# A decoder layer's self attention on one Trainium2 core: projection weights held while two batches' tokens stream

## The chip, the core and the metric

The kernel runs on one core of one Trainium2 chip. The metric is the device time of one execution in microseconds. Times named here are of one profiled execution unless the text says that they are the median of several runs.

## What is computed

One decoder layer in fp32 for 8 batches of 112 tokens of width 512: self attention, then cross attention over 375 context rows of width 128, then a mixture of experts, each behind a layer norm and each added to its input. Cut to what the change touches:

```python
def self_attention(x, Wq, Wk, Wv, Wp):          # x: [8, 112, 512], normed
    Q = (x @ Wq.T).reshape(B, T, 16, 32).transpose(0, 2, 1, 3)
    K = (x @ Wk.T).reshape(B, T, 4, 32).transpose(0, 2, 1, 3)
    V = (x @ Wv.T).reshape(B, T, 4, 32).transpose(0, 2, 1, 3)
    Q, K = apply_rope(Q), apply_rope(K)          # halves of 16: x1 cos - x2 sin, x2 cos + x1 sin
    scores = einsum('bkgtd,bksd->bkgts', Q.reshape(B, 4, 4, T, 32), K) / sqrt(32)
    attn = softmax(where(causal, scores, lowest))
    return einsum('bkgts,bksd->bkgtd', attn, V) -> [B, T, 512] @ Wp.T

def cross_attention(hidden, kv_c, Wq, w_kc_q, w_kc_kv, W_qr, W_kr, Wo):   # 16 heads
    q_big = einsum('bshk,hkq->bshq', hidden @ Wq.T, w_kc_q)
    scores = einsum(q_big @ W_qr, kv_rope @ W_kr)  # per head, over 375 context rows
    ...
```

## The kernel before

The engines' programs are written out by hand, one function per engine, and each engine runs its instructions in exactly the order of that function. They meet by semaphores only. The part around the change is the block of self attention, from about 10 to 165 us of the span. It runs in `ROUNDS` = 4 rounds; round i treats two batches, q = 0 and 1. The loop `for i in range(ROUNDS)` in each engine's program sets the order of the work.

**Projection.** Token rows are layer-normed (`first_norm`, L1613 on DVE gives `xn`), turned by PE (`turn_x`) into `xt_hl`: ACT copies a high part, DVE subtracts to get a low part. The weights `wqkv_hl` are split in the same way, and a product is three matmuls, high by high, high by low, low by high (`mm3`, L62 to L64). These operands have the type fp32r, a rounded fp32; other matmuls here take plain fp32, and one such instruction shows as two records in the profile. `project_qkv(i, q)` holds one batch's 112 tokens in the array and streams weights past them: 12 matmuls of 512 columns for the queries, 12 of 256 for keys and values. The results lie with tokens on partitions.

**Rotary embedding.** `rope` on DVE (L1634 to L1637, six multiplications a batch), `rope_add` on POOL (L2116, L2119, two additions of 512 elements a batch), then `turn_qk` turns queries and keys on PE (8 transposes a batch, L741), and ACT copies them to SBUF (`copy_qk`, L1234). ACT copies the values (`copy_v`, L1227).

**Scores and softmax.** `scores` adds the mask by a bf16 matmul (L824) and 16 matmuls on tiles of 32 rows (L829). On DVE `shift` takes the largest value (L1646) and subtracts it (L1648), ACT takes the exponential (`exp`, L1238), DVE sums (L1653), POOL normalises (L2126). A round's probabilities are used in the next round: `turn_probs` (L848, four groups of four transposes, ACT copies each, L1245), `apply_probs` (L858), `heads_high` on ACT (L1250) and `heads_low` on DVE (L1658) split the result, `project_out` (24 matmuls of 512 columns for both batches), `turn_x2` turns the next norm's output.

**Weights of the cross attention,** made in the same loop: round i treats the pairs of heads p = 2i and 2i+1. `scores_weight` (L750) gives `m_sb`, `out_weight` (L757) gives `bw_sb`, `query_weight` (L764) multiplies `m_sb` by the query weight, ACT copies the result (`at_sb`), `turn_query_weight` (L771) turns it on PE, and DVE or ACT copies it into `aw_sb`. `turn_context` (L778) and `context_turned_low` (L1684) prepare the context rows of one batch (`kvt_hl`).

Four PSUM banks hold scores and, between two scores, the weights of the cross attention (`s_ps`); `f_ps` (two banks) holds projections and their turned forms; `k_ps` (two banks, also `b_ps`) holds turned probabilities, heads and the output projection.

Of the kernel before, what the change touches and what calls it, by code (L numbers as in the profile page):

```python
# [12 lines left out]
F32 = mybir.dt.float32  # L13
F32R = mybir.dt.float32r
# [270 lines left out]
def attention(nc, a, sem, sb, ctx, ident, x_all, x_sb, xn2_hl, w_raw, p_raw, mask, stats_all, ow_dram, kvn_dram, kvt_dram, aw_dram,  # L285
# [30 lines left out]
    with ExitStack() as room:  # L316
        wqkv_hl = sb("wqkv_hl", [128, 2, KC, QKV], F32R, room)
        xt_hl, xn = pairs("xt_hl", [128, 2, KC, T], F32R, room), pairs("xn", [T, C], F32, room)
# [8 lines left out]
    with ExitStack() as room:  # L327
# [4 lines left out]
        at_sb, aw_sb, bw_sb = sb("at_sb", [128, C], F32, room), sb("aw_sb", [128, C], F32, room), sb("bw_sb", [128, 2, C], F32, room)  # L332
# [20 lines left out]
    with ExitStack() as room:  # L353
        qcos, qsin = sb("qcos", [T, HD], F32, room), sb("qsin", [T, HD], F32, room)
        mask_bf, ident_bf = sb("mask_bf", [T, PER, T], BF16, room), sb("ident_bf", [T, T], BF16, room)
        rq, rt = pairs("rq", [T, C], F32, room), pairs("rt", [T, C], F32, room)
        rk, rkt = pairs("rk", [T, GROUPS, PER, HD], F32, room), pairs("rkt", [T, 2, GROUPS, HD], F32, room)
        qt, kt = sb("qt", [128, KC, T], F32, room), sb("kt", [128, KC, T], F32, room)
# [18 lines left out]
    with ExitStack() as room:  # L377
        wp_hl, x2n = sb("wp_hl", [128, 2, KC, C], F32R, room), pairs("x2n", [T, C], F32, room)
        v_sb = [sb(f"v_sb{z}", [T, GROUPS, HD], F32, room) for z in range(4)]
# [49 lines left out]
    tab_loaded, mask_loaded, setup = sem("tab_loaded"), sem("mask_loaded"), sem("setup")  # L429
# [5 lines left out]
    at_done, at_copied, ta_done, a_ready = sem("at_done"), sem("at_copied"), sem("ta_done"), sem("a_ready")  # L435
# [10 lines left out]
    qkv_done, v_copied = sem("qkv_done"), sem("v_copied")  # L446
    rope_read, roped = sem("rope_read"), sem("roped")
    qkt_done, qkt_copied = sem("qkt_done"), sem("qkt_copied")
# [12 lines left out]

    def is_last(i):
        return i == ROUNDS

# [112 lines left out]
    with nc.Block() as block:  # L577
        @block.sync
        def _(sp):
# [53 lines left out]
            sp.dma_start(qcos[:, :], a["qcos"]).then_inc(tab_loaded, 16)  # L633
            sp.dma_start(qsin[:, :], a["qsin"]).then_inc(tab_loaded, 16)
# [12 lines left out]
            for p in range(PAIRS):  # L647
# [7 lines left out]
                if p + 1 < PAIRS:  # L655
                    sp.wait_ge(at_done, p + 1)
                    load_q(p + 1)
# [15 lines left out]
                if p == 5:  # L673
                    sp.wait_ge(a_stored, 16 * 4)
                    sp.wait_ge(qkv_done, 2 * B)
# [62 lines left out]
        def _(pe):  # L738
# [4 lines left out]

            def scores_weight(p):
# [14 lines left out]
            def query_weight(p):  # L759
# [8 lines left out]
            def turn_query_weight(p):  # L768
# [2080 lines left out]
```

## Time and profile before

| quantity | value |
|---|---|
| time, median of 3 runs (lowest, highest) | 562.0 us (561.52, 563.93) |
| profiled execution | 559.57 us, span 557.7 us |
| busy PE | 528.3 us (95%) |
| busy PEld (weight load) | 375.9 us |
| busy DVE | 400.5 us |
| busy ACT | 302.9 us |
| busy POOL | 281.3 us |
| mean granted clock of TensorE | 0.998 |

The span is the first to the last instruction; the execution's own time has 1.87 us around it. PE is busy for nearly all of the span, and its overlapped weight loads (PEld) are counted apart. In the table of 40 slices PE stands at 9 tenths or more in nearly all slices behind the first three. The self-attention block is slices 1 to 12.

### The profile page before, as it was taken

How to read it: one execution, taken by the hardware profiler on the slowest of the kernel's cores; microseconds unless marked ns; L12 is line 12 of the kernel's file. 1: busy time of each engine (PE TensorE's matmuls, PEld its weight loads, DVE VectorE, ACT ScalarE, POOL GpSimd, SP SyncE). 2: the span in 40 equal slices, each digit the busy share in tenths (PEclk: the TensorE clock that was granted, in tenths of full speed). 3: DMA queues.
4: the chain of work that ended last, by engine and by line, in shares of the span. 5: the costliest groups of instructions: out<-in, count | busy, mean ns of one | idle time of the engine just before them, and what ended most of it. 6: DMA issues, size and time to landing. Idle time of an engine off the chain costs nothing. (4 is left out here: it accounts for less than half of the span.)

```text
span 557.7 us, 9735 instructions
## 1 busy us (share of the span) xinstructions
PE 528.3 (95%) x3451; PEld 375.9 (67%) x3451; DVE 400.5 (72%) x912; ACT 302.9 (54%) x693; POOL 281.3 (50%) x359
## 2 busy tenths in 40 slices
PE   5989999999989999999999999999999999998996
PEld 4657776767767676576666776677678766884443
DVE  5675798797586698866877468894576667786873
ACT  3164735735655677655776456775466653622430
POOL 0579643564715776812666215693154552572650
PEclk9999999999999999999999999999999999999999
DMA  8976645766451630233693333244030019125828
GB/s 242 273 259 229 225 137 162 270 182 205 178 168 56 167 135 2 38 88 121 173 278 92 79 95 84 42 77 76 0 115 9 0 35 419 35 82 108 214 87 263
DMA packets 46194, 76.64 MB, mean 137 GB/s; under 512 B 20066, under 2 KB 30084, under 8 KB 45252
## 3 DMA queue, kind: packets, MB, share of 16 engines
q1 hardware_dynamic: 42948, 63.60, 36.8%
q0 software_dynamic: 2176, 10.60, 8.6%
q10 hardware_dynamic: 1024, 1.84, 1.0%
q8 instruction: 28, 0.46, 0.3%
q14 instruction: 18, 0.15, 0.1%
HBM read 57.36 MB, written 28.10 MB: 153 GB/s over the span
## 5 line engine op out<-in xcount | busy, mean ns | idle before, releaser
L2133 POOL TENSOR_TENSOR xprob<-xprob,erec 128x375 f32<-128x375 f32 x112 | 93.8, 843 | 129.4 <-DVE erec L1751 129.1
L1340 ACT ACTIVATE xprob<-s_ps,nmax 128x375 f32<-128x375 f32 x112 | 64.2, 573 | 55.0 <-DVE nmax L1746 53.2
L1746 DVE TENSOR_REDUCE nmax<-s_ps 128x1 f32<-128x375 f32 x112 | 59.5, 538 | 0.0
L2126 POOL TENSOR_TENSOR prob<-prob,rec 112x1792 f32<-112x1792 f32 x8 | 25.5, 3183 | 51.4 <-DVE rec L1654 51.2
L62 PE MATMUL s_ps<-kvt,qt_hl 128*128 128x376 f32 x112 | 48.1, 429 | 2.0 <-ACT xprob L1340 1.3
L1729 DVE SCALAR_TENSOR_TENSOR pt_hl<-f_ps,pt_hl 125x384 f16<-125x384 f32 (+1 forms) x62 | 38.0, 614 | 13.9 <-ACT pt_hl L1318 12.6
L62 PE MATMUL k_ps<-ow,ctx_hl 128*128 128x512 f16 (+1 forms) x104 | 39.6, 381 | 0.0
L64 PE MATMUL k_ps<-ow,ctx_hl 128*128 128x512 f16 (+1 forms) x104 | 39.4, 379 | 0.0
L63 PE MATMUL k_ps<-ow,ctx_hl 128*128 128x512 f16 (+1 forms) x104 | 39.4, 379 | 0.0
L63 PE MATMUL s_ps<-kvt,qt_hl 128*128 128x376 f32 x112 | 37.4, 334 | 0.0
L64 PE MATMUL s_ps<-kvt,qt_hl 128*128 128x376 f32 x112 | 37.4, 334 | 0.0
L1737 DVE SCALAR_TENSOR_TENSOR ctx_hl<-k_ps,ctx_hl 128x448 f16<-128x448 f32 (+1 forms) x32 | 18.7, 584 | 25.8 <-ACT ctx_hl L1326 23.6
L1318 ACT ACTIVATE pt_hl<-f_ps 125x384 f16<-125x384 f32 (+1 forms) x62 | 32.9, 535 | 6.1 <-PE f_ps L954 5.9
L954 PEld LDWEIGHTS f_ps<-ident,xprob 128*125 128x125 f32 x215 | 31.8, 186 | 4.4 <-DVE pt_hl L1729 1.3
L62 PE MATMUL k_ps<-pt_hl,kvn 125*128 125x448 f16 x96 | 34.1, 355 | 0.6 <-DVE pt_hl L1729 0.6
L954 PE MATMUL f_ps<-ident,xprob 128*125 128x128 f32 x215 | 34.2, 275 | 0.4
L63 PE MATMUL k_ps<-pt_hl,kvn 125*128 125x448 f16 x96 | 33.8, 352 | 0.0
L64 PE MATMUL k_ps<-pt_hl,kvn 125*128 125x448 f16 x96 | 33.8, 352 | 0.0
L62 PEld LDWEIGHTS s_ps<-kvt,qt_hl 128*128 128x128 f32 x112 | 21.2, 189 | 11.2 <-issue 6.3
L2139 POOL TENSOR_TENSOR qw<-qw_raw,qw 128x640 fp32r<-128x640 f32 x16 | 25.5, 1600 | 3.3 <-ACT qw L1346 3.2
L1751 DVE RECIPROCAL erec<-esum 128x1 f32<-128x1 f32 x112 | 17.5, 156 | 13.3 <-ACT xprob L1340 13.3
L2420 POOL DMA_INDIRECT done_dram<-o_sb,to x18 | 17.5, 970 | 16.7 <-DVE o_sb L2719 16.7
(380 smaller groups left out, 1499.7 us busy)
## 6 DMA issues: line engine op xcount, KB each, us to landing
w<-w_dram SPq DMA_DIRECT2D x6, 1024.0 KB, 10.0
raw_b<-in_raw SPq DMA_DIRECT2D x8, 640.0 KB, 5.5
raw_m<-in_raw SPq DMA_DIRECT2D x8, 576.0 KB, 4.6
raw_q<-in_raw SPq DMA_DIRECT2D x8, 512.0 KB, 7.1
ow_dram<-bw_sb SPq DMA_DIRECT2D x8, 512.0 KB, 5.8
ow_raw<-ow_dram SPq DMA_DIRECT2D x8, 512.0 KB, 3.2
qw_raw<-aw_dram SPq DMA_DIRECT2D x16, 256.0 KB, 3.0
w_dram<-in_w POOLq DMA_DIRECT2D x8, 512.0 KB, 5.8
```

The costliest lines, as they stand in the source:

```text
L62: pe.matmul(out, a_hl[0], b_hl[0], start=start, stop=False, skip_group_check=True)
L63: pe.matmul(out, a_hl[0], b_hl[1], start=False, stop=False, skip_group_check=True)
L64: return pe.matmul(out, a_hl[1], b_hl[0], start=False, stop=stop, skip_group_check=True)
L954: mm = pe.transpose(bank[0:LP, j * 128:(j + 1) * 128], xprob[slot(n - 1, k)][:, c * LP:(c + 1) * LP], ident[:, :])
L1318: act.activation(pt_hl[:, c, 0, turned_cols(part)], bank_of(n, name)[0:LP, 0:width(part)], ACT.Copy, scale=PSCALE).then_inc(high_copied, 1)
L1340: act.activation(xprob[z][:, 0:L], s_bank(n, k)[:, 0:L], ACT.Exp, bias=nmax[:, z:z + 1], accum_out=esum[:, z:z + 1]).then_inc(xexp_done, 1)
L1729: dve.scalar_tensor_tensor(pt_hl[:, c, 1, tok], bank_of(n, name)[0:LP, 0:width(part)], PSCALE, pt_hl[:, c, 0, tok], ALU.mult, ALU.subtract ...
L1737: dve.scalar_tensor_tensor(ctx_hl[q][:, 1, :, 0:own_t], heads[:, :, 0:own_t], 1.0 / PSCALE, ctx_hl[q][:, 0, :, 0:own_t], ALU.mult, ALU.sub ...
L1746: dve.tensor_reduce(nmax[:, z:z + 1], s_bank(n, k)[:, 0:L], X, ALU.max, negate=True).then_inc(xmax_done, 1)
L2126: pool.tensor_tensor(prob[q][:, :, :, :], prob[q][:, :, :, :], rec[q][:, :, :].unsqueeze(3).broadcast_to([T, PER, GROUPS, T]), ALU.mult).t ...
L2133: pool.tensor_tensor(xprob[z][:, 0:L], xprob[z][:, 0:L], erec[:, z:z + 1].broadcast_to([128, L]), ALU.mult).then_inc(xp_ready, 1)
L2139: pool.tensor_tensor(qw[:, i, 1, :], qw_raw[:, i, 1, :], qw[:, i, 0, :], ALU.subtract).then_inc(qw_low, 1)
```

## The change

Queries, keys and values are projected the other way around: 128 columns of a weight are held in the array, and the 224 tokens of both batches of a round stream past them. So `project_part` (L814) makes 72 matmuls of 224 columns a round in place of 48 (24 of 512, 24 of 256), and queries, keys and values come out turned, features on partitions. `project_q(i + 1)` (48 of them) stands where the projection of the next round's first batch stood, `project_kv(i)` (24) where that of the second batch stood. `xt_hl` is now one tile for both batches, and `wqkv_hl` holds the query columns in another order of heads.

- The rotary embedding works on the turned form: DVE multiplies by the cosine (L1668) and brings each half into the other's place by a shuffle across partitions (L1669), POOL multiplies by the sine and adds (L2141, L2142). A round has three such groups: queries of 448 elements twice, keys of 224 once. The tables come by two DMAs with each row four times, are turned on PE once (`turn_tables`) and copied by ACT.
- `turn_qk` and `copy_qk` go. The values have to be turned back: ACT copies them (`vt_sb`, L1273), `turn_v` makes two transposes (L846), ACT copies again (`v_sb`, L1279).
- `query_weight` makes its product turned, by 8 matmuls that stream 64 columns (L790), and `turn_query_weight`, `at_sb` and its copies go; the copies of `m_sb` and `aw_sb` are all on ACT (L1305, L1317).
- `masks` is split from `scores`. The four groups of `turn_probs` are split into two and two: for the first batch `turn_v` and `scores_weight` (M) stand between, and for the second batch two of the four mask matmuls.
- Three matmuls of `keep_busy` in round 0 go, five others stay.

```diff
+            def project_part(tiles, bank, k, first):
+                for j, m in enumerate(tiles):
+                    out = bank[:, j * 2 * T:(j + 1) * 2 * T]
+                    for n, (w, x) in enumerate(((0, 0), (0, 1), (1, 0))):
+                        mm = pe.matmul(out, wqkv_hl[:, w, k, m * 128:(m + 1) * 128], xt_hl[:, x, k, :],
+                                       start=(first and j == 0 and n == 0), stop=(k == KC - 1 and n == 2), skip_group_check=True)
+                return mm
...
+            def project_kv(i):
...
+                for z, done in ((0, qk_done), (1, vt_done)):
+                    pe.wait_ge(rope_read, 3 * i + z + 1)
+                    for k in range(KC):
+                        mm = project_part((PER + z,), f_ps[z], k, k == 0)
+                    mm.then_inc(done, 1)
+            def turn_v(i):
+                pe.wait_ge(vt_copied, i + 1)
+                for q in range(2):
+                    mm = pe.transpose(f_ps[1][0:T, 2 * T + q * 128:2 * T + (q + 1) * 128], vt_sb[:, q * T:(q + 1) * T], ident[:, :])
+                mm.then_inc(v_turned, 1)
...
-                for i in range(2):
-                    mm = pe.matmul(s_ps[i * XR:(i + 1) * XR, 3, :], m_sb[:, i * XR:(i + 1) * XR], wq[:, i],
-                                   start=True, stop=True)
-                mm.then_inc(at_done, 1)
...
                 for c in range(KC):
-                    mm = pe.transpose(s_ps[:, 0, c * 128:(c + 1) * 128], at_sb[:, c * 128:(c + 1) * 128], ident[:, :])
-                mm.then_inc(ta_done, 1)
+                    for i in range(2):
+                        o = c * 128 + i * XR
+                        mm = pe.matmul(s_ps[:, 0, o:o + XR], wq[:, i, c * 128:(c + 1) * 128], m_sb[:, i * XR:(i + 1) * XR],
+                                       start=True, stop=True, skip_group_check=True)
+                mm.then_inc(aw_done, 1)
...
@@ PE, order of a round
                 if i == 0:
                     scores_weight(p)
-                project_qkv(i, 1)
+                project_kv(i)
                 if i:
+                    turn_probs(i, 0, (0, 1))
+                    turn_v(i)
                     scores_weight(p)
+                    turn_probs(i, 0, (2, 3))
                 out_weight(p, 0)
-                if i:
-                    turn_probs(i, 0)
                 out_weight(p, 1)
...
                 turn_context(p)
-                turn_qk(i, 0)
-                turn_query_weight(p)
                 if i:
-                    turn_probs(i, 1)
+                    turn_probs(i, 1, (0, 1))
+                masks(i, 0, (3, 2))
+                if i:
+                    turn_probs(i, 1, (2, 3))
+                masks(i, 0, (1, 0))
                 scores(i, 0)
-                turn_qk(i, 1)
...
                 if more:
-                    project_qkv(i + 1, 0)
+                    project_q(i + 1)
...
+            def rope(i, z):
+                made, rest, n = roped_parts(i, z)
...
+                dve.tensor_tensor(made, src, qcos[:, :].unsqueeze(1).broadcast_to([128, n, T]), ALU.mult)
+                dve.stream_shuffle(rest, src, ROTATED).then_inc(rope_read, 1)
...
+            def rope_add(i, z):
...
+                own.link(pool.tensor_tensor(rest, rest, qsin[:, :].unsqueeze(1).broadcast_to([128, n, T]), ALU.mult))
+                pool.tensor_tensor(made, made, rest, ALU.add).then_inc(roped, 1)
```

**PE from the scores of a round's second batch on.** Before, `f_ps<-wqkv_hl,xt_hl` is the projection of the next round's second batch (its last row is shown), `raw_m` is `scores_weight`, `raw_b` `out_weight`, `ident,prob` `turn_probs`, `raw_q,m_sb` `query_weight`, and `rq`, `rk`, `at_sb` are what `turn_qk` and `turn_query_weight` turn.

```order
L64 MATMUL f_ps<-wqkv_hl,xt_hl 112x256
L750 MATMUL s_ps<-raw_m 128x64 x6
L757 MATMUL s_ps<-raw_b 128x512
L848 MATMUL k_ps<-ident,prob 112x112 x16
L757 MATMUL s_ps<-raw_b 128x512
L858 MATMUL k_ps<-probt,v_sb 32x112 x16
L764 MATMUL s_ps<-raw_q,m_sb 64x512 x2
L778 MATMUL s_ps<-ident,kvn_sb 128x125 x3
L741 MATMUL f_ps<-ident,rq 128x112 x4
L741 MATMUL f_ps<-ident,rk 128x112 x4
L771 MATMUL s_ps<-ident,at_sb 128x128 x4
```

In the change, with the semaphores that an instruction waits for, the same stretch begins:

```order
L814 MATMUL f_ps<-xt_hl,wqkv_hl 128x224 [waits rope_read]
L814 MATMUL f_ps<-xt_hl,wqkv_hl 128x224 x11
L814 MATMUL f_ps<-xt_hl,wqkv_hl 128x224 [waits rope_read]
L814 MATMUL f_ps<-xt_hl,wqkv_hl 128x224 x11
L888 MATMUL k_ps<-ident,prob 112x112 [waits p_ready]
L888 MATMUL k_ps<-ident,prob 112x112 x7
L846 MATMUL f_ps<-ident,vt_sb 112x128 [waits vt_copied]
L846 MATMUL f_ps<-ident,vt_sb 112x128
L774 MATMUL s_ps<-raw_m 128x64 [waits s_shifted,raw_m_loaded]
L774 MATMUL s_ps<-raw_m 128x64 x5
L888 MATMUL k_ps<-ident,prob 112x112 [waits pt_copied]
L888 MATMUL k_ps<-ident,prob 112x112 x3
```

The projection of keys and values (24 instructions) and two of four groups of turns come first; then `turn_v`, which waits for ACT's copy `vt_copied`, stands ahead of `scores_weight`, which stood directly behind the projection before.

**ACT at the same place,** before: `prob<-prob` is `exp` of a round's second batch, and the rows behind it belong to the next round.

```order
L1238 ACTIVATE prob<-prob 112x1792
L1227 COPY v_sb<-f_ps 112x128
L1245 COPY probt<-k_ps 112x448 x4
L1266 COPY bw_sb<-s_ps 128x512
L1283 ACTIVATE kvn_sq,squares<-kvn_sb 125x384
L1266 COPY bw_sb<-s_ps 128x512
L1250 CAST ot_hl<-k_ps 128x448
L1276 COPY at_sb<-s_ps 128x512
L1293 CAST kvt_hl<-s_ps 128x375
```

In the change:

```order
L1283 ACTIVATE prob<-prob 112x1792
L1273 COPY vt_sb<-f_ps 128x224
L1291 COPY probt<-k_ps 112x448 x2
L1279 COPY v_sb<-f_ps 112x256
L1305 COPY m_sb<-s_ps 128x128
L1291 COPY probt<-k_ps 112x448 x2
L1312 COPY bw_sb<-s_ps 128x512
L1324 ACTIVATE kvn_sq,squares<-kvn_sb 125x384
L1312 COPY bw_sb<-s_ps 128x512
L1317 COPY aw_sb<-s_ps 128x512
```

The copy of the turned values, for which `turn_v` waits, is behind `exp` in ACT's program, where `copy_v` was. The copies of queries and keys are gone, and those of `m_sb` and `aw_sb` have come in.

**POOL at the start of round 0,** before: the last operation on the context, then `rope_add` of two batches.

```order
L2107 TENSOR_TENSOR kvn_sb<-kvn_sb,rot_t 125x384
L2116 TENSOR_TENSOR rq<-rq,rt 112x512
L2119 TENSOR_TENSOR rk<-rkt 112x512
L2116 TENSOR_TENSOR rq<-rq,rt 112x512
L2119 TENSOR_TENSOR rk<-rkt 112x512
L2103 TENSOR_TENSOR kvn_sb<-ctx_raw,kcos 125x384
```

In the change:

```order
L2129 TENSOR_TENSOR kvn_sb<-kvn_sb,rot_t 125x384
L2141 TENSOR_TENSOR turned<-turned,rope_tables 128x448
L2142 TENSOR_TENSOR qt<-qt,turned 128x448
L2141 TENSOR_TENSOR turned<-turned,rope_tables 128x448
L2142 TENSOR_TENSOR qt<-qt,turned 128x448
L2141 TENSOR_TENSOR turned<-turned,rope_tables 128x224
L2142 TENSOR_TENSOR kt<-kt,turned 128x224
L2125 TENSOR_TENSOR kvn_sb<-ctx_raw,kcos 125x384
```

Four operations of 512 elements became four of 448 and two of 224, and the first scores wait for all of them.

## Rows read from the trace of the kernel before

**Rows 1.** Windows by round: us, busy us (count) per engine, PEclk, DMA share, GB/s.

```profile
49.26:87.36 38.10, 36.81 (x330) 27.37 (x326) 31.86 (x53) 21.55 (x43) 24.20 (x17) 1.00 0.57 180
...
125.51:162.41 36.90, 34.75 (x311) 25.27 (x307) 25.11 (x44) 21.98 (x42) 18.17 (x13) 1.00 0.53 177
```

**Rows 2.** Waits of PE, 20 to 165 us: line, releaser, us in total, times, longest.

```profile
PE k_ps L848 <- ACT probt L1245: 2.0, 7, 0.3
PE s_ps L824 <- DVE kvt_hl L1684: 1.5, 2, 0.8
PE k_ps L741 <- DVE x2n L1596: 1.5, 1, 1.5
...
PE s_ps L771 <- ACT at_sb L1276: 0.2, 1, 0.2
```

**Rows 3.** Timeline of PE in round 1: start us, us, instruction, count, idle before.

```profile
49.59 0.39 PE L63 MATMUL f_ps<-wqkv_hl,xt_hl 128*112 128x512 f32 x1
49.82 0.40 PE L64 MATMUL f_ps<-wqkv_hl,xt_hl 128*112 128x512 f32 x1
...
52.38 0.28 PE L64 MATMUL f_ps<-wqkv_hl,xt_hl 128*112 128x256 f32 x1
52.49 0.28 PE L62 MATMUL f_ps<-wqkv_hl,xt_hl 128*112 128x256 f32 x1
...
53.63 1.52 PE L750 MATMUL s_ps<-raw_m 128*128 128x64 f32 x12
54.99 1.08 PE L757 MATMUL s_ps<-raw_b 128*128 128x512 f32 x2
...
59.82 1.08 PE L764 MATMUL s_ps<-raw_q,m_sb 128*64 128x512 f32 x4
60.83 0.54 PE L778 MATMUL s_ps<-ident,kvn_sb 125*128 125x125 f32 x3
61.20 0.55 PE L741 MATMUL f_ps<-ident,rq 112*128 112x112 f32 x4
...
61.97 0.60 PE L771 MATMUL s_ps<-ident,at_sb 128*128 128x128 f32 x4
62.41 0.93 PE L848 MATMUL k_ps<-ident,prob 112*112 112x112 f32 x8
```

**Rows 4.** Timeline of PE in the experts' part: the gate's matmuls.

```profile
479.17 0.95 PE L2436 MATMUL e_ps<-gate,xt 128*112 128x8 f32 x8
479.98 0.45 PE L62 MATMUL s_ps<-xn_hl,sw_hl 128*128 128x448 f32 x1
```

**Rows 5.** Timeline of DVE after the scores of a round's second batch.

```profile
87.50 2.02 DVE L1646 TENSOR_REDUCE top<-s_ps 112x16 f32<-112x1792 f32 x1 [0.63 <-PE s_ps L829]
89.56 2.02 DVE L1648 TENSOR_TENSOR prob<-s_ps,top 112x1792 f32<-112x1792 f32 x1
```

**Rows 6.** Timeline of ACT at the same place.

```profile
91.62 1.70 ACT L1238 ACTIVATE prob<-prob 112x1792 f32<-112x1792 f32 x1 [5.22 <-DVE prob L1648]
93.22 0.25 ACT L1227 COPY v_sb<-f_ps 112x128 f32<-112x128 f32 x1
```

**Rows 7.** Timeline of DVE in the middle of round 1.

```profile
60.62 0.62 DVE L1658 TENSOR_TENSOR ot_hl<-k_ps,ot_hl 128x448 fp32r<-128x448 f32 x1 [1.21 <-ACT ot_hl L1250]
61.16 2.60 DVE L1613 TENSOR_SCALAR xn<-x_all,mean,rstd 112x512 f32<-112x512 f32 x2
```

**Rows 8.** Timeline of POOL at the start of round 0.

```profile
25.99 1.06 POOL L2107 TENSOR_TENSOR kvn_sb<-kvn_sb,rot_t 125x384 f32<-125x384 f32 x1
27.01 1.26 POOL L2116 TENSOR_TENSOR rq<-rq,rt 112x512 f32<-112x512 f32 x1
```

**Rows 9.** Timeline of PE: the first scores.

```profile
31.61 1.05 PE L829 MATMUL s_ps<-kt,qt 32*112 32x112 f32 x32
```

**Rows 10.** Timeline of PE at the kernel's start: warming matmuls, twice.

```profile
5.47 4.09 PE L888 MATMUL s_ps<-ident 128*128 128x128 f32 x18 [5.47 <-DMA ident<-in_ident]
...
10.96 1.91 PE L888 MATMUL s_ps<-ident 128*128 128x128 f32 x16
```

More of the change, by code:

```diff
@@ L742, in turn, with turn_tables @@
                 mm.then_inc(done, 1)
+            def turn_tables():
+                pe.wait_ge(tables_ready, 32)
+                for n in range(2):
+                    mm = pe.transpose(b_ps[0][:, n * T:(n + 1) * T], tables[:, n].rearrange("t r d -> t (r d)"), ident[0:T, 0:T])
+                mm.then_inc(tables_ready, 1)
             def scores_weight(p):
@@ new lines, in project_q @@
+            def project_q(i):
+                pe.wait_ge(xt_low, 2 * i + 2)
+                if i == 0:
+                    for k in range(KC):
+                        pe.wait_ge(wqkv_low, k + 1)
+                        for z in range(2):
+                            mm = project_part((2 * z, 2 * z + 1), f_ps[z], k, k == 0)
+                            if k == KC - 1:
+                                mm.then_inc(qk_done, 1)
+                    return
+                for z in range(2):
+                    for k in range(KC):
+                        mm = project_part((2 * z, 2 * z + 1), f_ps[z], k, k == 0)
+                    mm.then_inc(qk_done, 1)
@@ new lines, in project_kv @@
+            def project_kv(i):
+                if i == 0:
+                    pe.wait_ge(wqkv_low, KC + 1)
+                for z, done in ((0, qk_done), (1, vt_done)):
+                    pe.wait_ge(rope_read, 3 * i + z + 1)
+                    for k in range(KC):
+                        mm = project_part((PER + z,), f_ps[z], k, k == 0)
[5 more added lines that the diff above has]
+                mm.then_inc(v_turned, 1)
@@ L817, in scores, with masks @@
+            def masks(i, q, js):
+                b = 2 * i + q
+                if js[0] == PER - 1:
+                    pe.wait_ge(b_copied, 2 * b + 2)
                 if b == 0:
                     pe.wait_ge(setup, 2)
-                for j in reversed(range(PER)):
+                for j in js:
                     if j == 1:
@@ L1184, in _ @@
                     turn_x2(i, 1)
-                turn_query_weight(p + 1)
+                masks(i, 1, (3, 2, 1, 0))
                 scores(i, 1)
-            turn_probs(ROUNDS, 0)
+            turn_probs(ROUNDS, 0, (0, 1, 2, 3))
             query_pair(0, 1)
@@ L1238, in exp, with copy_probs @@
                 act.activation(prob[q][:, :, :, :], prob[q][:, :, :, :], ACT.Exp, scale=SCALE).then_inc(s_exp, 1)
-            def copy_probs(i, q):
+            def copy_probs(i, q, js=range(PER)):
                 c = 2 * (i - 1) + q
-                wait(act, pv_done, c)
-                for j in range(PER):
+                if js[0] == 0:
+                    wait(act, pv_done, c)
+                for j in js:
                     act.wait_ge(pt_done, 4 * c + j + 1)
@@ L1528, in _ @@
                 copy_out_weight(p + 1, 1)
-                if more:
-                    copy_v(i + 1, 0)
-                else:
+                if not more:
                     pair_high(0, 0)
```

243 lines of the change are left out of this document (105 added, 138 removed).

## The prediction

> **What bounds the kernel now.** I read the windows of the rounds first. A full round takes 38.10 us and PE is busy for 36.81 of them at a granted clock of 1.00; DVE, the next, has 31.86 [rows 1]. So PE bounds this part, and two things count: what PE has to do, and where it stands still. PE's waits between 20 and 165 us are seven lines that add up to 8.2 us, from 2.0 us in seven short waits for copies of turned probabilities down to 0.2 us; the longest single one is 1.5 us, for the next norm (`x2n`) [rows 2]. There is little to win from waits, and a new one is paid in full. The timeline of PE gives the price of each block, and the timelines of DVE, ACT and POOL show what a moved instruction will have to wait for.
>
> **Price of a projection matmul.** The split matmuls start 0.23 us apart at 512 columns and 0.115 at 256 [rows 3], so a batch costs 12 x 0.233 + 12 x 0.1165 = 4.19 us and a round 8.39. Both are 0.455 ns a column; by columns alone 224 would take 0.102 us. But what is held now has 128 columns, and it changes with every instruction. The nearest rows are `scores_weight`: 12 records of 64 columns with 128 held take 1.36 us, 0.113 each [rows 3], and the gate: 8 records of 8 columns with 112 held take 0.81 us, 0.101 each [rows 4]. Hardly any of that is streaming, so loading what is held sets a floor of about 0.112 us at 128 columns. I take 0.112, since it lies above the 0.102 of the columns. The bounds are 0.102 and, if load and stream don't overlap fully, 0.12.
>
> The Trainium skill (TensorE: Matmul & The Clock Gate, section Back-to-back issue gap) gives columns/2.4 + 2.5 ns for a warm matmul, 96 ns for 224 columns; by that alone 288 matmuls would take 4.6 us less than at 0.112 us. The same page's section LDWEIGHTS gives columns held/1.2 ns, 107 ns for 128 and 93 for 112. The trace speaks for the second as the limit here: 113 and 101 ns [rows 3, 4]; on the first it differs too, 0.233 us at 512 columns against the page's 216 ns.
>
> **PE's work in a full round.**
> - Projections: 72 x 0.112 = 8.06 for 8.39 us, -0.3.
> - Query weight, twice a round: 8 instructions, 16 records of 64 columns with 128 held, the shape of `scores_weight`, so 16 x 0.112 = 1.79 for 1.01 (59.82 to 60.83) [rows 3]: +1.56 for two. Without `turn_query_weight` (0.44 each, 61.97 to 62.41 [rows 3]): -0.88.
> - `turn_qk`, 0.77 us for the first batch (61.20 to 61.97 [rows 3]); with the gap between its halves I take 0.9 for the second, an estimate: -1.7. `turn_v` adds two transposes, +0.2.
>
> Together -1.1 us. In round 3, which no longer projects queries, it is 2.69 for 4.19, so -2.3.
>
> **The new wait.** Behind the scores of a round's second batch PE now runs 24 projections (2.69 us) and two of four groups of turns (8 at 0.096 by the 0.77 us of 8 turns [rows 3], 0.77 us), then meets `turn_v`. That waits for ACT's copy, and the copy stands behind `exp` in ACT's program. By the rows of before the scores end at 87.36; DVE takes 2.02 us twice from 87.50 [rows 5], ACT starts `exp` at 91.62 and is free at 93.22; a copy of 224 elements lies between 0.25 us for 128 and 1.70 for 1,792 [rows 6], by line 0.33. So the values are there at 93.55, and PE at 87.36 + 2.69 + 0.77 = 90.82: a wait of **2.7 us in rounds 1, 2 and 3**. `scores_weight`, the other turns and the output weight, all ready, are queued behind it. Before, the same chain lay under a projection of 4.19 us and blocks that did not need it. Nothing excludes that it grows a little where DVE is late with the subtraction; it falls to 0 only if `exp` were done 2.7 us earlier, which nothing in the change brings about.
>
> **Smaller waits, rounds 1 to 3.** The second group of the second batch's turns waits for the low part of the heads: a copy of 448 elements on ACT (0.53 by the same line) and 0.62 on DVE [rows 7], with 0.37 of `turn_context` and 0.38 of turns between: between 0 and 0.8, I take 0.5. The second pair of masks waits for the low part of the context, which on DVE is queued behind two norms of 2.60 us together [rows 7]: between 0 and 1.2, I take 0.4 as the block ahead of it on PE is shorter by `turn_qk`. Two short waits for copies of turns, 0.3 each [rows 2], go because other work now stands between: -0.6. The wait for `x2n` in round 3 [rows 2] hangs on DVE's own chain, so a PE that comes later waits less: -1.2 of 1.5.
>
> **Round 0.** There `turn_v` stands behind the output weights and waits for nothing. But the first scores wait for POOL: it is free for the rotation at 27.01 [rows 8], and 512 elements take 1.26, so 448 about 1.1 and 224 about 0.6: 4 x 1.1 + 2 x 0.6 + 0.2 between = 5.8, to 32.8. The scores started at 31.61 [rows 9]: +1.2. Then the projection of the next round's queries, 48 x 0.112 = 5.38, stands where one batch's 4.19 stood: +1.2, and the second query weight costs 0.78 - 0.44: +0.3. What was removed ahead of the first scores, and the three `keep_busy` matmuls, lies inside POOL's time and counts nothing.
>
> **At nothing.** DVE loses multiplications and gains shuffles; ACT loses eight small copies and gains two to four; both had idle time [rows 1]. The shuffle has no row; priced as a copy it is about 0.5 us for 448 elements, and at twice that it would add 0.5 us a round while PE still has the query weight to do, which is the cover. The two table loads have more packets and stand on SP's queue ahead of x, mask and the first weights: between 0 and the 1 us by which PE waits longer for the first weights; I take 0.
>
> **Sum.** Round 0 +2.7; rounds 1 and 2 each -1.1 + 2.7 + 0.5 + 0.4 - 0.6 = +1.9; round 3 -2.3 + 2.7 + 0.5 + 0.4 - 0.6 - 1.2 = -0.5. Together **+6.0 us**, and the rest of the kernel moves along, as it begins when PE gets there. The profiled execution took 559.57 us, so 565.6; it lies 2.4 us under the median of the runs (562.0), so the forecast for a median is **568.0 us**, 1.1% slower. Its own range is 565 to 571.
>
> **The rivals.**
> - *Columns set the pace* (0.102 us). For it: 512 and 256 columns run at exactly one rate [rows 3]. Against: the load-bound rows. 288 x 0.010 = 2.9 us less work, but the key and value block ends 0.24 earlier and three pauses grow by 0.7 in all: +3.8, **565.8**. Chance 0.14.
> - *Faster, because the new pause takes the place of the old waits.* Work falls by 4 x 1.1 = 4.5 in all, and if everything that PE waited for (8.2 us [rows 2]) comes in during the three pauses (8.1), the kernel gains: -4.5 + 8.1 - 8.2 = -4.6, **557.4**. For it: an engine that stands still lets the others catch up. Against: the waits for context and norm come from DVE's chains later in the round, not from values. It decides where over 6.4 of the 8.2 us go. Chance 0.20, somewhat over half of that faster by more than 0.5%.
> - *The clock falls in the pauses.* 2.7 us is longer than any wait of before here (1.5 [rows 2]); that one lies in a window at 1.00 [rows 1]. At the start 18 warming matmuls took 4.09 us and 16 of the same later 1.91 [rows 10], 0.227 against 0.119, the lower and the higher of the two levels. One such stretch costs 2.0 us; behind each of three pauses 6.0: **574.0**. Chance 0.08.
> - *The narrow matmul isn't fast.* No row shows a split matmul under 256 columns. If it went at the pace of plain fp32, `out_weight` tells the price: 1.08 us for 512 columns [rows 3], 0.92 without its tail of 0.16, so 0.40 for 224. 288 x 0.29 = 84 us, less the three pauses that it would cover: **644**. Chance 0.05, for all that speaks for it is the missing row.
>
> **How the numbers follow.** The forecast has 0.53. The range 559 to 574 leaves out the slow-matmul case, half of the clock case and the faster half of the gain, some 0.18. About 0.5% (2.8 us) is what a measurement of this kernel can tell from no change. Faster by over 0.5%: 0.12, from the gain. Within 0.5%: 0.08 from the gain, 0.05 from the columns, 0.04 from the forecast's lower edge: 0.17. Slower: the rest, 0.71.
>
> **What would show it.** In the profile after: the projection matmuls start 0.11 us apart (0.10 would be the first rival, 0.4 the last); PE waits at the transposes of `vt_sb` three times for ACT, 2 to 3 us each, and `exp` is what ACT did just before; query weight blocks of 1.8 us; the first scores wait for POOL; granted clock 1.00 in all rounds. If those waits are under 1 us, or if PE's other waits in this part fall from 8 to 2 us, the forecast is wrong.

## The result and the profile after

The change makes the kernel slower: a median of 575.43 us (571.21 to 578.54, 4 runs) against 562.96 (561.52 to 566.24, 4 runs), a ratio of 1.0208 with a 95% interval of 1.0125 to 1.0291. The forecast was 568.0 with a range up to 574. The direction was right, the size was half of what came.

The runs of the changed kernel differ more than those of before, and the longer ones have the lower mean granted clock: 0.986 at 571.21 us, 0.981 at 574.44, 0.982 at 576.43, 0.972 at 578.54, where all runs of before that the later comparisons list have 0.992 to 1.000. Ratios in this document leave out runs over 1.5% above the fastest of the same kernel, which in the changed kernel, where long runs go with a low clock, can make a ratio too small. The profiled execution is the one of 571.21 us: span 569.4 for 557.7, mean clock 0.986 for 0.998.

PE's waits from 20 to 175 us, columns as in [rows 2]; the shorter ones are left out:

```profile
PE f_ps L846 <- ACT vt_sb L1273: 7.6, 3, 2.5
PE s_ps L860 <- DVE kvt_hl L1704: 2.7, 4, 1.0
PE s_ps L868 <- POOL kt L2142: 1.6, 1, 1.6
PE k_ps L888 <- DVE ot_hl L1688: 1.4, 3, 0.5
...
PE s_ps L774 <- DVE prob L1678: 0.9, 1, 0.9
...
```

The new wait is there as forecast: three times 2.5 us at `turn_v`, for ACT's copy. ACT in round 1 makes that copy directly behind `exp`:

```profile
57.06 1.70 ACT L1283 ACTIVATE prob<-prob 112x1792 f32<-112x1792 f32 x1 [3.55 <-DVE prob L1678]
58.67 0.33 ACT L1273 COPY vt_sb<-f_ps 128x224 f32<-128x224 f32 x1
```

So are the waits for POOL ahead of the first scores (1.6) and for the heads (3 x 0.5). The first scores also wait longer for the context, 1.0. The first and the last of POOL's six operations for them, columns as in [rows 8]:

```profile
27.82 1.13 POOL L2141 TENSOR_TENSOR turned<-turned,rope_tables 128x448 f32<-128x448 f32 x1
...
33.15 0.66 POOL L2142 TENSOR_TENSOR kt<-kt,turned 128x224 f32<-128x224 f32 x1
```

Timeline of PE in rounds 0 and 1, columns as in [rows 3]:

```profile
42.02 5.92 PE L814 MATMUL f_ps<-xt_hl,wqkv_hl 128*128 128x224 f32 x48
47.77 1.90 PE L790 MATMUL s_ps<-m_sb,raw_q 128*128 128x64 f32 x16
...
52.81 2.94 PE L814 MATMUL f_ps<-xt_hl,wqkv_hl 128*128 128x224 f32 x24
55.59 0.93 PE L888 MATMUL k_ps<-ident,prob 112*112 112x112 f32 x8
59.05 0.67 PE L846 MATMUL f_ps<-ident,vt_sb 128*112 128x128 f32 x2 [2.53 <-ACT vt_sb L1273]
59.51 2.66 PE L774 MATMUL s_ps<-raw_m 128*128 128x64 f32 x12
61.97 1.70 PE L888 MATMUL k_ps<-ident,prob 112*112 112x112 f32 x8
63.46 3.01 PE L781 MATMUL s_ps<-raw_b 128*128 128x512 f32 x4
66.30 1.89 PE L790 MATMUL s_ps<-m_sb,raw_q 128*128 128x64 f32 x16
```

48 projection matmuls take 5.75 us (42.02 to 47.77) and 24 take 2.78, 0.116 to 0.120 each; a query weight takes 1.74. All of that is near the forecast (0.112 with a bound of 0.12, and 1.79). What isn't: behind the pause at 59.05 the 12 records of `scores_weight` take 2.46 us (59.51 to 61.97) where [rows 3] have 1.36 and the four output-weight records 2.84. The same instructions behind the same pause in round 3:

```profile
141.70 0.43 PE L846 MATMUL f_ps<-ident,vt_sb 128*112 128x128 f32 x2 [2.53 <-ACT vt_sb L1273]
141.97 1.45 PE L774 MATMUL s_ps<-raw_m 128*128 128x64 f32 x12
143.25 0.93 PE L888 MATMUL k_ps<-ident,prob 112*112 112x112 f32 x8
144.02 1.90 PE L781 MATMUL s_ps<-raw_b 128*128 128x512 f32 x4
145.76 1.89 PE L790 MATMUL s_ps<-m_sb,raw_q 128*128 128x64 f32 x16
```

Here `scores_weight` takes 1.28 us and the output weights 1.74. The windows, columns as in [rows 1], show the reason; the first is the stretch behind round 0's first scores, then comes, for round 1, the stretch from the scores to the pause's end, and for rounds 1, 2 and 3 the one behind the pause:

```profile
34.80:39.30 4.50, 3.60 (x21) 2.39 (x14) 4.21 (x3) 2.23 (x5) 3.52 (x7) 0.62 0.72 286
52.80:59.00 6.20, 3.72 (x36) 3.49 (x32) 4.89 (x6) 2.65 (x5) 2.65 (x4) 0.99 0.49 172
59.00:66.30 7.30, 7.25 (x26) 5.64 (x27) 2.07 (x2) 3.25 (x8) 7.30 (x3) 0.54 0.28 81
...
101.10:106.90 5.80, 5.76 (x27) 3.92 (x28) 2.06 (x2) 3.55 (x9) 3.75 (x3) 0.71 0.34 105
...
141.70:147.60 5.90, 5.90 (x45) 4.88 (x46) 2.02 (x2) 3.89 (x10) 3.85 (x3) 1.00 0.77 256
```

Behind the pause of round 1 the granted clock is 0.54 for 7 us, behind that of round 2 0.71 for 6 us, which is half speed (1.2 for 2.4 GHz) in most of it; behind that of round 3 it is 1.00. In round 0 it is 0.62 behind the wait for POOL.

Where the time came from, by the start of what follows each of the eight scores (us, both profiled executions):

| scores of round, batch | 0, 0 | 0, 1 | 1, 0 | 1, 1 | 2, 0 | 2, 1 | 3, 0 | 3, 1 |
|---|---|---|---|---|---|---|---|---|
| before | 32.6 | 49.3 | 66.3 | 87.4 | 104.5 | 125.5 | 142.6 | 162.4 |
| after | 34.8 | 52.8 | 73.5 | 94.9 | 114.1 | 135.5 | 153.0 | 171.3 |
| added since the one ahead | +2.2 | +1.3 | +3.6 | +0.3 | +2.1 | +0.3 | +0.4 | -1.5 |

The first half of a round, which holds the pause, costs 0.4 us more than before in round 3, where the clock stays up, and 3.6 and 2.1 in rounds 1 and 2, where it falls: with round 3 as the measure, 4.9 us of the 8.9 are the clock. The other 2.8 us of the 11.7 come behind the eighth scores, 2.5 of them from the gate of the experts' part on ([rows 4]; 479.17 before, 488.38 here), in instructions that the change does not touch. In every later profile, those of the code of before with an added wait too, the time behind the eighth scores is 1.6 to 6.9 us longer than in the one shown of before. That points at the execution of before, which was 3.4 us under the median, but no run tests it.

### The profile page after: what moved, and what is told of

It reads as the page before. It is cut to its first block and busy times, and to the rows that moved or that the text cites. A ratio compares the mean times of both kernels' runs of the same rounds, so it can differ in the third digit from the quotient of the medians.

```text
span 569.4 us, 9881 instructions
## 1 busy us (share of the span) xinstructions
PE 530.4 (93%) x3551; PEld 390.6 (69%) x3554; DVE 396.2 (70%) x895; ACT 295.6 (52%) x677; POOL 284.4 (50%) x367
## 5 line engine op out<-in xcount | busy, mean ns | idle before, releaser
L814 PE MATMUL f_ps<-xt_hl,wqkv_hl 128*128 128x224 f32 x288 | 35.1, 280 | 0.5 <-DVE turned L1669 0.5
L814 PEld LDWEIGHTS f_ps<-xt_hl,wqkv_hl 128*128 128x128 f32 x288 | 33.0, 192 | 2.3 <-issue 2.0
```

Of the source, the lines that this page charges most:

```text
L814: mm = pe.matmul(out, wqkv_hl[:, w, k, m * 128:(m + 1) * 128], xt_hl[:, x, k, :], start=(first and j == 0 and n == 0), stop=(k == KC - 1 a ...
```

## The experiments

Theory A is the forecast's: work and waits alone. Theory B: behind a pause TensorE's clock falls, and the slow stretch costs about as much again. Each ratio is to the kernel before on the same chip; it can differ a little from the quotient of the medians given with it.

**Fill the pause, shorten nothing.** The waits stay, but PE runs 12 unused bf16 matmuls in them.

```diff
-                    turn_probs(i, 0, (0, 1))
+                    turn_probs(i, 0, (0,))
+                    keep_busy(b_ps[1], 12)
+                    turn_probs(i, 0, (1,))
                     turn_v(i)
```

> The changed kernel with 12 bf16 matmuls of 448 columns (0.19 us each, 2.3 us together, results unused) put into PE's pause ahead of the turn of the values in rounds 1 to 3, into a bank that is free there. The wait itself stays as long: the values are no earlier. Theory A (only work and waits, as forecast): no change against the changed kernel, 575 us, ratio to before 1.020. Theory B (behind a pause of 2.5 us TensorE's clock falls, and the slow stretch costs as much again): granted clock 1.00 in rounds 1 to 3 and 3 to 6 us less, 569 to 572 us, ratio 1.010 to 1.016, with a smaller spread of the runs.

Measured: ratio 1.0108 (1.0069 to 1.0147), median 571.08 against 563.36. Timeline of PE in its round 2, then the windows behind the filled pause in rounds 1, 2 and 3:

```profile
101.36 2.43 PE L933 MATMUL k_ps<-mask_bf,ident_bf 112*112 112x448 bf16 x12
...
104.43 0.43 PE L846 MATMUL f_ps<-ident,vt_sb 128*112 128x128 f32 x2 [0.26 <-ACT vt_sb L1275]
104.70 1.45 PE L774 MATMUL s_ps<-raw_m 128*128 128x64 f32 x12
```

```profile
63.80:70.00 6.20, 6.20 (x66) 5.17 (x68) 1.78 (x2) 4.11 (x11) 6.20 (x2) 1.00 0.43 109
...
104.70:111.00 6.30, 6.30 (x70) 5.28 (x72) 1.75 (x2) 4.21 (x11) 4.44 (x3) 1.00 0.44 111
...
143.60:150.00 6.40, 6.40 (x74) 5.29 (x72) 1.72 (x2) 4.18 (x11) 4.56 (x3) 1.00 0.83 237
```

The values are no earlier, and the clock is 1.00 in all three. Theory A says 1.020; the run has half of that excess. What is left is 6.1 us by the ratio (3.9 to 8.3 by its interval) and 7.7 by the medians; the forecast's sum of work and waits, 6.0, lies in that range.

**The same pause in the kernel before.** Two places: ahead of the second half of a projection, and behind `scores_weight`.

```diff
                 for lo, hi, bank in ((0, C, 0), (C, QKV, 1)):
+                    if i and q == 1 and bank == 1:
+                        pe.wait_ge(s_exp, 2 * i)
```

> The kernel before with one added wait: in rounds 1 to 3 PE waits for the exponential of the round before ahead of the second half of the projection (keys and values of the second batch), a pause of about 3 us at the place where the change has one. Theory A: 3 x 2.9 less two short waits for turns that it covers, +8 us, ratio 1.014. Theory B: the clock falls behind it as in the changed kernel, +11 to +14 us, ratio 1.020 to 1.025, granted clock about 0.5 for several us behind each pause.

Measured: ratio 1.0214 (1.0152 to 1.0276). In time that is theory B's figure, but not by its mechanism. Timeline of PE in round 0 (a wait that is not the added one) and in round 2, and the windows behind the pauses of rounds 1, 2 and 3:

```profile
27.28 3.65 PE L757 MATMUL s_ps<-raw_b 128*128 128x512 f32 x4 [3.46 <-DMA raw_b<-in_raw]
...
100.34 0.37 PE L62 MATMUL f_ps<-wqkv_hl,xt_hl 128*112 128x256 f32 x1 [2.95 <-ACT prob L1240]
```

```profile
59.30:66.00 6.70, 6.46 (x48) 4.89 (x52) 4.00 (x9) 2.52 (x6) 4.45 (x3) 1.00 0.27 88
...
100.40:107.00 6.60, 6.31 (x44) 4.84 (x44) 4.05 (x9) 2.33 (x6) 4.30 (x2) 1.00 0.27 89
...
141.70:149.00 7.30, 7.01 (x72) 5.44 (x76) 3.96 (x9) 3.11 (x9) 5.09 (x3) 1.00 0.54 133
```

The pause is 3.0 us and the clock behind it 1.00, in all three rounds; each costs its 3 us and no more. The profiled execution is 15.4 us over that of before: 9.2 from the three pauses, 3.7 in round 0, where PE waited 3.5 us for a load, and 2.4 behind the eighth scores. So a pause of 3 us alone did not bring the clock down in this execution, and theory B in its simple form fell here. The longer wait for the load, which also stands directly behind wide projections, did: the clock is 0.50 from 28 to 30 us, and the four records behind it take 3.49 us (27.28 to 30.77) where those behind the pause of round 3 in the changed kernel take 1.74. So length counts too. One of the four runs, which has no profile, took 579.92 us at a mean clock of 0.980, the others 573.81 to 574.97 at 0.991 to 0.997; where the clock fell in that one is not known.

```diff
                     scores_weight(p)
+                    pe.wait_ge(s_rec, 2 * i)
                 out_weight(p, 0)
```

> The kernel before with one added wait in rounds 1 to 3, behind the product that makes M: PE waits for the sums of the round before (DVE), a pause of about 2.4 us that, unlike that of the run with the wait inside the projection, is followed by plain fp32 products and turns, as the pause of the change is. Theory A: +2.4 x 3 less the two short waits for turns, +6.5 us, ratio 1.011. Theory B1 (a pause of this length brings the clock down wherever it lies): +6.5 and 1 to 4 us more. Theory B2 (it depends on what runs around it, and falls here, where the pause inside the projection hardly did): low clock behind at least one of the three, +10 us or more, ratio 1.017 or above.

Measured: ratio 1.0198 (1.0113 to 1.0282). The wait, and the windows behind its three places:

```profile
PE s_ps L757 <- DVE rec L1655: 7.4, 3, 2.5
```

```profile
56.80:63.00 6.20, 5.88 (x44) 3.57 (x48) 2.07 (x8) 2.89 (x6) 5.92 (x4) 0.73 0.15 61
...
99.00:106.00 7.00, 6.44 (x64) 3.90 (x65) 3.08 (x10) 4.53 (x11) 6.71 (x5) 1.00 0.26 62
...
139.80:147.00 7.20, 6.63 (x66) 4.08 (x67) 2.71 (x9) 4.71 (x12) 6.90 (x5) 1.00 0.70 201
```

Three waits of 2.5 us; the clock falls behind the first (0.73) and not behind the other two. By its terms that is theory B2's result, by one pause of three. In these two profiles it fell behind 1 pause of 6, in the changed kernel behind 2 of 3. Two more runs set the mix around the pause against its length.

In the first the changed kernel keeps its pause, and the wide output weights come directly behind it.

```diff
                     turn_v(i)
-                    scores_weight(p)
-                    turn_probs(i, 0, (2, 3))
+                    wait(pe, s_shifted, p)
                 out_weight(p, 0)
                 out_weight(p, 1)
+                if i:
+                    scores_weight(p)
+                    turn_probs(i, 0, (2, 3))
```

> The changed kernel with the same pause of 2.5 us and the same work, but the order behind the pause changed in rounds 1 to 3: the output weights (instructions that stream 512 columns) come directly behind the turn of the values, and the product for M (64 columns each) and the second pair of turns after them. Theory B1 (the pause alone): the clock falls as in the changed kernel, ratio 1.018 to 1.021. Theory B2 (pause and a stretch of narrow matmuls and turns together): the clock stays at 1.00 behind most of the pauses, ratio 1.009 to 1.013.

Measured: ratio 1.0246 (1.0189 to 1.0302). Windows behind the three pauses:

```profile
59.00:64.00 5.00, 4.97 (x19) 2.92 (x20) 2.05 (x2) 1.12 (x3) 5.00 (x3) 0.66 0.00 0
100.00:104.00 4.00, 3.96 (x10) 1.94 (x10) 2.06 (x2) 1.13 (x3) 1.95 (x2) 0.57 0.00 0
140.00:146.00 6.00, 5.41 (x23) 3.54 (x24) 2.27 (x2) 1.94 (x6) 3.93 (x3) 0.72 0.55 173
```

The clock falls behind all three and the ratio lies above both theories, so wide output weights behind the pause did not keep it up; B2 fell in that half.

In the second the kernel before gets a pause with the change's neighbours: turns ahead of it, M and turns behind. In the cut below, the second argument of `turn_probs` picks its groups of turns, as in the changed kernel.

```diff
                 if i:
+                    turn_probs(i, 0, (0, 1))
+                    pe.wait_ge(s_rec, 2 * i)
                     scores_weight(p)
+                    turn_probs(i, 0, (2, 3))
                 out_weight(p, 0)
-                if i:
-                    turn_probs(i, 0)
                 out_weight(p, 1)
```

> The kernel before with the mix of the change around an added pause in rounds 1 to 3: projection, two of four groups of turns, a wait for the sums of the round before (pause of about 3.3 us), then the product for M, the other turns, and only then the output weights. Theory B1: as the run with a pause of 3.0 us inside the projection, where the clock stayed up three times in three: +10 us less the short waits for turns, ratio 1.017, no low clock in rounds 1 to 3. Theory B2: the clock falls behind two or three of the pauses, another 4 to 10 us, ratio 1.023 or more.

Measured: ratio 1.0329 (1.0274 to 1.0383), 579.72 us. The wait, and the windows behind its three places:

```profile
PE s_ps L750 <- DVE rec L1656: 9.4, 3, 3.1
```

```profile
58.20:64.00 5.80, 5.79 (x32) 4.27 (x36) 1.92 (x7) 1.89 (x4) 5.76 (x4) 0.71 0.36 105
100.00:108.00 8.00, 7.36 (x40) 5.54 (x44) 2.51 (x9) 2.26 (x6) 7.33 (x6) 0.57 0.24 74
144.00:152.00 8.00, 7.59 (x37) 5.46 (x41) 2.28 (x9) 2.37 (x6) 7.56 (x6) 0.57 0.55 173
```

3.1 us, and the clock falls each time; with 3.0 us between wide projections it fell not once in the profile. The mean clocks of all runs agree: 0.978 to 0.983 in the four here, 0.991 to 0.997 in three of the four there. The code and the length are all but the same, the neighbours on both sides are not. The run before this one speaks against the side behind. No run changes the side ahead alone, but round 0 has a wait with no turns directly ahead: for a load, between the projection of keys and values and the output weights. Timeline of PE there in two further runs, first the one with five edits to the changed kernel described below, then this one:

```profile
25.50 3.13 PE L781 MATMUL s_ps<-raw_b 128*128 128x512 f32 x4 [2.25 <-DMA raw_b<-in_raw]
...
25.59 1.98 PE L757 MATMUL s_ps<-raw_b 128*128 128x512 f32 x4 [2.06 <-DMA raw_b<-in_raw]
```

Behind the change's projections of 224 columns, 2.25 us were enough (clock 0.57 from 26 to 30 us); behind those of 256 columns, 2.06 us were not (1.00), where 3.46 us had been. So turns directly ahead are not needed: the narrower projection itself may count, and so may the length.

**The changed kernel again, and with the old query weight.**

> The changed kernel once more, on the same chip as the runs sent with it. Both theories: 572 to 577 us, ratio to before 1.015 to 1.025. Theory B also: waits of about 2.5 us at the turn of the values in rounds 1 to 3, the same in every profile, but behind another of them the clock falls than in the first profile (there it fell in rounds 1 and 2 and not in 3), and runs with a lower mean clock are longer by about their lost share of the clock.

Measured: median 577.35 us of four runs (569.91 to 583.31) against 562.19, ratio 1.0179 (1.0074 to 1.0283). In its profile, of the longest run, the three waits at `turn_v` are 2.5 us each again, and the windows behind them show 0.56, 0.59 and 0.77: round 3 was hit too this time.

```profile
66.70:74.50 7.80, 7.80 (x31) 5.73 (x32) 1.94 (x2) 3.77 (x10) 7.80 (x4) 0.56 0.27 76
108.80:116.50 7.70, 7.66 (x33) 6.15 (x33) 2.06 (x2) 3.65 (x10) 5.57 (x6) 0.59 0.25 79
150.70:158.00 7.30, 7.30 (x41) 5.51 (x42) 2.01 (x2) 4.10 (x10) 5.25 (x5) 0.77 0.64 203
```

With the run with the wide instructions behind the pause and the one that follows, the clock fell behind 11 of 12 pauses in the changed kernel's code.

```diff
-                for c in range(KC):
-                    for i in range(2):
-                        o = c * 128 + i * XR
-                        mm = pe.matmul(s_ps[:, 0, o:o + XR], wq[:, i, c * 128:(c + 1) * 128], m_sb[:, i * XR:(i + 1) * XR], ...)
+                for i in range(2):
+                    mm = pe.matmul(s_ps[i * XR:(i + 1) * XR, 3, :], m_sb[:, i * XR:(i + 1) * XR], wq[:, i], start=True, stop=True)
+                mm.then_inc(at_done, 1)
...
                 turn_context(p)
+                turn_query_weight(p)
```

> The changed kernel with the query weight made as before: 2 instructions of 512 columns, copied, turned by 4 transposes, copied (all copies on ACT). Both theories price the new way at 1.79 us for 1.01 + 0.44 on PE, eight times, so this run should save 8 x 0.34 = 2.7 us of PE's work, up to 4.4 where it also shortens later waits: 571 to 573 us, ratio 1.013 to 1.017, if the clock does as in the changed kernel.

Measured: ratio 1.0188 (1.0102 to 1.0274). The saving can't be seen: it is smaller than what the clock takes in one run and not in the next (mean clock 0.975 to 0.983). Inconclusive in time; the price stands on the blocks of the trace, 1.74 us against 1.01 and 0.44.

**Shorten the pause.** ACT copies the values ahead of the exponential.

```diff
-                copy_turned_v(i)
+                if i == 0:
+                    copy_turned_v(i)
...
                 out_squares(p + 1)
                 if more:
+                    copy_turned_v(i + 1)
                     exp(i, 1)
```

> The changed kernel with ACT's copy of the turned values moved ahead of the exponential, PE's order unchanged. The wait at the turn of the values goes; PE then stops at the second pair of turns, whose banks ACT empties only behind the exponential, about 1.3 us. Theory A: 1.2 us less in three rounds, 3.6 in all, 571 to 572 us, ratio 1.014. Theory B: if 1.3 us is too short to bring the clock down, another 3 to 6 us less, 566 to 569 us, ratio 1.005 to 1.010.

Measured: ratio 1.0094 (1.0059 to 1.0129), median 569.81. The ratio is theory B's, but not by its mechanism. The wait at `turn_v` is gone; PE stops for 0.44 us at M and 0.53 at the turns instead, and behind that the clock still fell in rounds 1 and 2 of its profile (0.50 from 106 to 108 us), not in round 3. Between projection and output weights there are then only turns and the narrow product for M, so in two rounds of three even short stops in such a stretch went with a fall.

```diff
                     turn_v(i)
                     scores_weight(p)
+                    out_weight(p, 0)
                     turn_probs(i, 0, (2, 3))
-                out_weight(p, 0)
+                else:
+                    out_weight(p, 0)
```

> As the run with the values copied first, and one output-weight product (0.9 us) moved ahead of the second pair of turns, so that PE has 6.1 us of work behind the scores and the turns are ready at about 6.5. Pause under 0.5 us. Theory A: the three pauses of 2.5 us less 0.4 go, 6.5 us in all, 569 us, ratio 1.010. Theory B: the slow stretches go as well, 563 to 566 us, ratio 1.000 to 1.005, and granted clock 1.00 in rounds 1 to 3.

Measured: four runs between 559.62 and 574.40 us, too far apart for a ratio. The profiled one has a span of 563.0 and no slow stretch in rounds 2 and 3, but a new wait of 2.5 us in round 1, for POOL, and a low clock behind it (0.70 from 70 to 74 us). Inconclusive in time; in rounds 2 and 3 the profile is B's.

**All of it together.** The values first, the output weight as cover, the old query weight, and in round 0 the sine part and the addition of the first of three rotation groups on DVE and 16 warming matmuls in place of 5.

```diff
             rope(0, 1)
+            rope_add_dve(0, 0)
...
-            rope_add(0, 0)
...
-                    keep_busy(b_ps[0], 5)
+                    keep_busy(b_ps[0], 16)
```

> The changed kernel with four edits: values copied ahead of the exponential, an output-weight product ahead of the second pair of turns, the first scores' rotation shared between POOL and DVE with 16 warming matmuls in place of 5 behind them, and the query weight made as before. Theory A: pauses -6.5, query weight -3, round 0 -1: 575 - 10.5 = 564.5 us, ratio 1.003. Theory B: no slow stretches behind the pauses and in round 0 either, 557 to 561 us, ratio 0.990 to 0.997, mean clock 0.995 or more.

Measured: ratio 1.0014 (0.9978 to 1.0049), median 563.73 against 562.19. That is theory A's figure; B's is missed because the clock still fell in round 0 and once in round 1, behind a wait for POOL. The changed kernel had no wait of that kind; that its pause had hidden it is the likely reason. PE's waits and POOL's timeline:

```profile
PE k_ps L892 <- POOL prob L2172: 3.5, 3, 2.8
```

```profile
57.95 0.66 POOL L2167 TENSOR_TENSOR turned<-turned,rope_tables 128x224 f32<-128x224 f32 x1 [2.91 <-DVE turned L1688]
...
59.31 4.60 POOL L2255 TENSOR_TENSOR wp_hl<-p_raw,wp_hl 128x2048 fp32r<-128x2048 f32 x1
63.88 3.17 POOL L2172 TENSOR_TENSOR prob<-prob,rec 112x1792 f32<-112x1792 f32 x1
```

POOL stands 2.9 us for the rotation of keys, which DVE makes only behind the shift; behind that come 4.6 us for the output projection's weights and only then the probabilities that PE wants. The next edit turns the two around:

```diff
                     rope_add(i + 1, 1)
-                    rope_add(i + 1, 2)
                 if i == 0:
                     pool.wait_ge(wp_high, 1)
                     pool.tensor_tensor(wp_hl[:, 1], p_raw[:, :, :], wp_hl[:, 0], ALU.subtract).then_inc(wp_low, 1)
+                if more:
+                    rope_add(i + 1, 2)
```

> The run with four edits and a fifth: on POOL, the low part of the output projection's weights (4.6 us) goes ahead of the rotation of round 1's keys, for which POOL waited 2.9 us, so that the probabilities of round 0's second batch are normalised about 3 us earlier and PE's wait for them in round 1 (2.8 us) goes. Theory A: 2.8 us less, 561 us, ratio 0.996. Theory B: the slow stretch behind that wait goes as well, 558 to 560 us, ratio 0.992 to 0.996.

Measured: ratio 0.9972 (0.9943 to 1.0000), median 562.64 against 564.53. The same row of its waits:

```profile
PE k_ps L892 <- POOL prob L2172: 1.0, 3, 0.3
```

Of 2.8 us 0.3 are left, and the clock is 1.00 in rounds 1 to 3; it fell in round 0, behind a load and behind the first scores. In time the run lies near 0.996, where the two theories meet, and does not tell them apart. Filling the waits of round 0 too:

```diff
+                    keep_busy(b_ps[1], 10)
                     out_weight(p, 0)
...
-                    keep_busy(b_ps[0], 16)
+                    keep_busy(b_ps[0], 22)
```

> The run with five edits, and more warming matmuls in round 0: 10 ahead of the output weights, where PE waits 0 to 4 us for a load, and 22 in place of 16 behind the first scores. Theory A: no gain, or up to 1 us lost where the load is early, ratio 0.997 to 0.999. Theory B: in the profile of the run with five edits the clock fell behind both waits in round 0, at a price of some 3 us, so 1 to 3 us less, ratio 0.991 to 0.995.

Measured: ratio 0.9975 (0.9947 to 1.0003), median 561.72 against 563.72, mean clock 0.994 to 1.000 in 12 runs. In its profile the attention part ends 4.1 us sooner than in that of before. The ratio is theory A's, although the clock stayed up (0.999 in the profile). The gain of 2 us in the whole is within what can't be told from none: the version is level with before, not faster.

**All pauses of the changed kernel filled,** without any other edit (12 matmuls in each pause and 16 behind the first scores):

> The changed kernel with the 12 warming matmuls in each pause ahead of the turn of the values and 16 in place of 5 behind the first scores; no work is taken away and no wait is shortened. Theory A: 575 us as the changed kernel, ratio 1.018 to 1.020. Theory B: mean clock 0.993 or more, and 567 to 569 us, ratio 1.006 to 1.011, near the 568 us of the forecast, which priced the waits and left the clock at 1.

Measured: ratio 1.0101 (1.0072 to 1.0131), 570.37 against 564.53, +5.8 us. The ratio is theory B's; the clock still fell in two places of its profile, behind the wait for POOL in round 0 and behind one of 1.6 us for the context in round 1, so that the mean of the four runs is 0.987 to 0.995, where theory B wanted 0.993 or more.

## Why the prediction was wrong in size

- **The matmul's price** was within its bounds: 0.116 to 0.120 us for a forecast of 0.112 with a bound of 0.12. That fits the load of what is held as the limit, which no run varied; columns alone (the first rival, 0.102) fell, and so did the slow narrow matmul.
- **The new wait** was right in place, cause and size: 2.5 us for 2.7, three times, with `exp` ahead of the copy on ACT.
- **The smaller waits** were partly right: heads 0.5 as forecast; the wait for the context did not come in the first halves of rounds 1 to 3, and the one in the second halves, 0.76 before, became 0.4. So a full round without a fall of the clock costs +0.7 (0.4 and 0.3 in the table), not +1.9.
- **Round 0** came to +3.5 for a forecast of +2.7, +2.2 for +1.2 up to the first scores and +1.3 for +1.5 behind them. POOL began the rotation at 27.82 us, not at the 27.01 of [rows 8], for the most part because the load of the context rows let it start 0.7 us later; its six operations took 6.0 us for 5.8. That what was removed "counts nothing" held for the time up to the scores, but it had also kept PE at work there: without it PE stood 1.0 and 1.6 us ahead of the scores, and behind them the clock fell (0.62 from 34.8 to 39.3 us). In this profile that cost little, as PE then still waited 0.9 us for DVE.
- **The clock** is the step that failed. The forecast left it at 1.00 and gave its fall in the pauses a chance of 0.08, because the longest wait of before, 1.5 us, was not followed by a lower clock. The runs showed 0.54 and 0.71 behind two of the three pauses: in the profile the fall costs 4.9 us in two rounds, and filling the pauses takes the ratio from 1.0208 to 1.0108, some 5 to 6 us (the intervals of the two overlap), and leaves about what the forecast had summed. That +6.0 fits the filled kernel is in part luck, as rounds were priced too high and round 0 and the part behind the eighth scores too low. For the same reason it is in part luck that the clock's price as a rival, 574.0 us, is close to the measured 575.4: it had the clock fall three times at 2.0 us each on top of the 6.0.
- **The faster rival** fell: PE's waits in this part add up to 16.9 us, 9.3 beside the new ones, where it needed the old 8.2 to go (8.4 as the seven rows of that view add up).

The runs with an added wait show why the rows of before misled: among its wide projections the clock stayed up through three pauses of 3 us, and the change both makes a pause and puts other work ahead of it, turns and a projection in narrower matmuls. Shown is that filling the changed kernel's pauses keeps the clock at 1.00 behind them and gives back about half of the loss, and that a pause of one length can bring the clock down in one place and not in another. That the neighbours decide at this length rests on one profile of three pauses on either side (a wait of 3.5 us for a load, behind wide projections too, did bring the clock down); which of them and how much is not settled, and neither is why the same pause of the changed kernel was without a fall once in twelve. What makes the part behind the eighth scores 1.6 to 6.9 us longer in the later profiles than in the first was not tried.

## What to carry to other kernels

A pause of 2 to 3 us on TensorE had two prices here: its length, and what the clock took behind it. The second was about as large as the first (4.9 us behind two pauses of 2.5), varied from run to run, and came mostly where turns or narrower matmuls stood around the pause; a few unused wide matmuls put into the pause tell in one run whether another kernel pays it. And an operation that is removed as pure cost may have been cover: before it goes, look at which wait it lies in.

## What the runs showed of the hardware

- The same instructions behind the same wait of 2.53 us ran at a clock of 0.54, 0.71 and 1.00 in three rounds of one execution, and at 0.56, 0.59 and 0.77 in another.
- In the code of before, pauses of 3.0 us between wide projection matmuls left the clock at 1.00 three times out of three in one profile, while a wait of 3.5 us behind such matmuls brought it to 0.50 there, and pauses of 3.1 us with turns ahead, M and turns behind were followed by 0.71, 0.57 and 0.57 in another.
- A split matmul with 224 columns that stream past 128 held ones took 0.116 to 0.120 us, as much as 256 columns past 112 (0.11 to 0.12 [rows 3]), though it streams fewer.
